# Tiles of a pair of source blocks and one target block in a graph network kernel, a dense stage without GpSimd, and other warm matmuls in the sort

## The reference, cut to what matters

```python
for l in range(5):                                   # L0
    h = leaky(x @ W1[l] + b1[l]) @ W2[l] + b2[l]
    e = leaky(edge_attr_32 @ We1[l] + be1[l]) @ We2[l] + be2[l]
    agg = segment_sum(h[src] * e * dot_scale[l], dst)
    x = layernorm(x + agg * res_w[l]) * ln_g[l] + ln_b[l]
# L1: rst = segment_sum((x * deg_out**-0.5) @ W [src], dst) * deg_in**-0.5 + bias
# L2 twice: softmax over the edges of a target, of q[dst].k[src], times v[src]
# last: segment_sum(relu(x[src] + edge_attr_64), dst)
```

## Time and profile before

| | us |
|---|---|
| median of 3 runs (8425.77 to 8462.65) | 8448.33 |
| the profiled execution, its own time | 8526.05 |
| its span | 8524.4 |

### The profile page before, as it was taken

How to read it: one execution, slowest core, us unless ns; L and a number is a source line. 1 busy time by engine, 2 the same in 40 slices (tenths; PEclk the granted TensorE clock), 3 DMA queues, 4 the chain that set the end, 5 groups by cost and what they waited for, 6 DMA issues and landing times. The chain is left out here.

```text
span 8524.4 us, 285239 instructions
## 1 busy us (share of the span) xinstructions
PE 6618.3 (78%) x79417; PEld 5068.7 (59%) x79424; DVE 6072.1 (71%) x17993; ACT 3076.6 (36%) x5080; POOL 3765.3 (44%) x5536
## 2 busy tenths in 40 slices
PE   5999999934444588788788787887777999999787
PEld 3555655623333467576566666665675777677676
DVE  7444444479999798789788798898554554455799
ACT  2443434412222444344343343343222333233344
POOL 2655666644443255355354454454994000000354
PEclk9888888865555798789798898888555999899999
DMA  3655555622222677577576576675232111111476
GB/s 85 168 163 158 164 163 164 168 54 56 57 57 56 193 174 176 129 176 175 131 175 165 139 175 151 154 175 145 104 116 84 67 64 44 60 69 63 109 191 168
DMA packets 1739057, 1083.39 MB, mean 127 GB/s; under 512 B 1256693, under 2 KB 1623980, under 8 KB 1729274
## 3 DMA queue, kind: packets, MB, share of 16 engines
q1 hardware_dynamic: 1105530, 739.41, 29.9%
q0 software_dynamic: 254336, 267.05, 13.7%
q10 hardware_dynamic: 379008, 74.48, 4.9%
HBM read 812.49 MB, written 266.72 MB: 127 GB/s over the span
## 5 line engine op out<-in xcount | busy, mean ns | idle before, releaser
L540 POOL DMA_DIRECT2D big<-rows x3384 | 1819.6, 538 | 3258.7 <-issue 2189.2
L1307 PE MATMUL ps<-big 128*128 128x64 bf16 x27072 | 1722.9, 204 | 528.8 <-DVE big L1753 312.8
L1307 PEld LDWEIGHTS ps<-big 128*128 128x128 bf16 x27072 | 1330.2, 102 | 890.4 <-issue 624.6
L810 POOL DMA_INDIRECT rows<-big x800 | 1007.6, 1260 | 754.3 <-ACT big L938 409.0
L1295 PE MATMUL ps<-big 128*128 128x64 bf16 x27072 | 1098.2, 202 | 102.2 <-DVE big L1768 41.3
L1295 PEld LDWEIGHTS ps<-big 128*128 128x128 fp8e4 x27072 | 988.6, 104 | 202.0 <-issue 145.5
L1034 ACT CAST big<-big 128x512 bf16<-128x512 f32 x940 | 581.2, 618 | 1153.5 <-DVE big L1781 1153.5
L1559 DVE SCALAR_TENSOR_TENSOR big<-big 128x1000 f32<-128x1000 f32 (+1 forms) x300 | 359.1, 1197 | 860.0 <-ACT big L923 603.5
L1040 ACT CAST big<-big 128x512 bf16<-128x512 f32 x1128 | 697.2, 618 | 586.6 <-issue 436.2
L1781 DVE TENSOR_TENSOR big<-ps,big 128x512 f32<-128x512 f32 x940 | 645.8, 687 | 275.2 <-PE ps L1295 261.8
L1256 PE MATMUL ps<-identb,big 128*128 128x128 bf16 x1504 | 341.4, 301 | 563.1 <-DVE big L1669 561.5
(11 more groups left out here) (259 smaller groups left out, 10337.1 us busy)
## 6 DMA issues: line engine op xcount, KB each, us to landing
big<-ohsD SPq DMA_DIRECT2D x564, 256.0 KB, 2.9
big<-ohdD SPq DMA_DIRECT2D x564, 256.0 KB, 3.5
big<-rows POOLq DMA_DIRECT2D x3384, 32.0 KB, 2.8
big<-rows SPq DMA_DIRECT2D x3384, 32.0 KB, 2.4
big<-maskD SPq DMA_DIRECT2D x50, 1600.0 KB, 6.6
big<-rows ACTq DMA_DIRECT2D x2256, 32.0 KB, 2.5
big<-keyT SPq DMA_DIRECT2D x100, 488.3 KB
maskD<-big SPq DMA_DIRECT2D x25, 1600.0 KB, 6.1
```

Of the source, the lines that this page charges most:

```text
L540: eng.dma_start(edge[:, s.r, j, :], rows[bass.ds(v[s.r * (hi - lo) + j - lo], P), col]).then_inc(landed[s.r], 16)
L810: pool.indirect_dma_start(out=rows[:, :], out_offset=bass.IndirectOffsetOnAxis(ap=sidx[0:EP, j, c:c + 1], axis=0), in_=stage[0:EP, j, c, : ...
L1307: last = pe.matmul(pacc[:, bass.ds(w[j], D)], hot[:, g.r, j * P:(j + 1) * P], parts[:, g.r, c, j * D:(j + 1) * D], start=False, stop=False ...
```

## The change

- **Tiles.** A bucket is now a pair of source blocks (VP = 13 pairs) and one target block. The formula for TILES gives 1152, so NG is 144 and there are 36 trips. The source id of an edge is its number among 256, and `ohS` is 256 columns wide (`iota1b` too). A table slice has 384 columns (two blocks by three parts); `tabq` gets a 26th block of zeros. A gather has two source one-hots per tile: 48 matmuls a group, in sums of six.
- **Counting.** TensorE turns both halves of `ohS` and multiplies 256 columns of counts per tile, which VectorE adds as 256 columns. The eight PSUM banks serve one group, so that each half waits for the same half of the group before. ScalarE makes four copies of 512 columns per group, with four semaphore counts. `ohD` has two buffers, not four. The first KEEP = 5 target one-hots of a group are stored and loaded, and MADE = 3 are remade.
- **Dense stage.** `find_over` goes to ScalarE as Relu(count - 65534), ahead by two block rows. VectorE multiplies that by the excess and adds it (one instruction), and the mask is the smaller of ln(2 count + tiny) and 1e28 times it; `make_far` goes. ScalarE keeps the even turns of a block row and VectorE the odd ones.
- **Sort.** One wide matmul of zeros ahead of each of the five outputs of a step, and twelve ahead of the first one in every fourth step; `be2p` is zeroed and the bias matmul goes over all 128 rows.

```diff
+VP = -(-W // 2)
+W2 = 2 * VP
+TILES = -(-((E + VP * W * (P - 1)) // P + VP * (QUAD - 1)) // 32) * 32
+KEEP = 5
+MADE = GT - KEEP
...
-        cmat = carve(W * W * P, dt=U16)
+        cpad = carve((W * W + 1) * P, dt=U16)
+        cmat = cpad[:, 0:W * W * P]
-        ohS = carve(2, GT, P, dt=BF16)
-        ohD = carve(RING, GT, P, dt=BF16)
-        ohsT = carve(2, GT * P, dt=U8)
+        ohS = carve(2, GT, 2 * P, dt=BF16)
+        ohD = carve(2, GT, P, dt=BF16)
+        ohsT = carve(2, 2 * GT * P, dt=U8)
...
-                sp.wait_ge(ohs_kept, i * 2 + 2)
+                sp.wait_ge(ohs_kept, i * 4 + 4)
...
-                sp.wait_ge(hots_ready, i * 2 + 1)
+                sp.wait_ge(hots_ready, i * 2 + 2)
...
-                             ohD[:, r, 0:QUAD, :].rearrange("p a b -> p (a b)")).then_inc(dst_stored[r], 16)
+                             ohD[:, r % 2, 0:KEEP, :].rearrange("p a b -> p (a b)")).then_inc(dst_stored[r % 2], 16)
...
-                sp.dma_start(hot[:, s.r:s.r + 2, 0:QUAD * P], ohdD[bass.ds(s.i, 2)].rearrange("g p f -> p g f")).then_inc(hot_loaded[s.r // 2], 16)
+                sp.dma_start(hot[:, s.r:s.r + 2, 0:KEEP * P], ohdD[bass.ds(s.i, 2)].rearrange("g p f -> p g f")).then_inc(hot_loaded[s.r // 2], 16)
...
+            def find_over(w, c):
+                act.wait_ge(craw_loaded[w % RAW], 16 * (w // RAW + 1))
+                if w >= 2:
+                    act.wait_ge(cfull_made, (w - 2) * CUTS + c + 1)
+                span = slice(c * CW, (c + 1) * CW)
+                act.activation(over_full[w % 2][:, span], craw[w % RAW][:, span], ACT.Relu, bias=step2[:, 2:3]).then_inc(over_made, 1)
+
...
-                act.activation(lnc[w % 2][:, span], cfull[w % 2][:, span], ACT.Ln, bias=tiny[:, 0:1]).then_inc(ln_made, 1)
+                act.activation(lnc[w % 2][:, span], cfull[w % 2][:, span], ACT.Ln, scale=2.0, bias=tiny[:, 0:1]).then_inc(ln_made, 1)
...
+                    elif w + 2 < W:
+                        find_over(w + 2, k - CUTS)
...
-                    for _ in range(12 if m == 0 else 0):
-                        pe.matmul(bank(4), zerob[:, :], each(iota1b[:, :], 4), start=True, stop=True)
-                    pe.matmul(to, onesb[0:3, 0:EP], be2p[0:3, p, :], start=True, stop=False, skip_group_check=True)
+                    for _ in range(12 if m == j == 0 else 1):
+                        pe.matmul(bank(4 + h), zerob[:, :], each(iota1b[:, 0:P], 4), start=True, stop=True)
+                    pe.matmul(to, onesb[:, 0:EP], be2p[:, p, :], start=True, stop=False, skip_group_check=True)
...
-                    if past(i, 2):
-                        pe.wait_ge(ohs_kept, i * 2 + (h - 3))
-                        pe.wait_ge(c_added[4 * h + 3], i - 1)
+                    if past(i, 1):
+                        pe.wait_ge(ohs_kept, i * 4 + (2 * h - 2))
+                        pe.wait_ge(c_added[4 * h + 3], i)
                     for j in range(4):
                         m = 4 * h + j
-                        pe.matmul(bank((r % 2) * 2 + h)[:, j * P:(j + 1) * P], ohS[:, r % 2, m, :], identb[:, :], start=True, stop=True)
-                        last = pe.matmul(bank(4 + (r % 2) * 2 + h)[:, j * P:(j + 1) * P], ohD[:, r, m, :], ohS[:, r % 2, m, :], start=True, stop=True)
+                        for k in range(2):
+                            pe.matmul(bank(2 * h + k)[:, j * P:(j + 1) * P], ohS[:, r % 2, m, k * P:(k + 1) * P], identb[:, :], start=True, stop=True)
+                        last = pe.matmul(bank(4 + 2 * h + j // 2)[:, j % 2 * 2 * P:(j % 2 + 1) * 2 * P], ohD[:, r % 2, m, :], ohS[:, r % 2, m, :], start=True, stop=True)
...
-                            for c in range(3):
-                                last = pe.matmul(pG[g.r][:, j * D:(j + 1) * D], ohsR[:, g.r, j * P:(j + 1) * P].bitcast(F8),
-                                                 slices[:, g.r, q // QUAD, c * D:(c + 1) * D], start=(c == 0), stop=(c == 2))
+                            for k in range(2):
+                                at = ((q // QUAD * 2 + k) * QUAD + j - q) * P
+                                for c in range(3):
+                                    last = pe.matmul(pG[g.r][:, j * D:(j + 1) * D], ohsR[:, g.r, at:at + P].bitcast(F8),
+                                                     slices[:, g.r, q // QUAD, (3 * k + c) * D:(3 * k + c + 1) * D],
+                                                     start=(k + c == 0), stop=(k + c == 3))
...
-                    if past(i, RING):
-                        dve.wait_ge(dst_stored[r], t * 16)
+                    if past(i, 2):
+                        dve.wait_ge(dst_stored[r % 2], t * 32 + 16 * (r // 2))
...
-                    own = cmat[:, bass.ds(two[r % 2 * GT + m] * P, P)]
+                    own = cpad[:, bass.ds(two[r % 2 * GT + m] * P, 2 * P)]
...
-                        last = dve.tensor_copy(slices[:, s.r, q, :], flat(tabq)[:, bass.ds(names[s.r * 2 + q], 3 * D)])
+                        last = dve.tensor_copy(slices[:, s.r, q, :], flat(tabq)[:, bass.ds(names[s.r * 2 + q], 6 * D)])
...
-                dve.tensor_tensor(lnc[w % 2][:, span], lnc[w % 2][:, span], far[w % 2][:, span], ALU.min).then_inc(mask_done, 1)
+                dve.scalar_tensor_tensor(lnc[w % 2][:, span], lnc[w % 2][:, span], STEEP, lnc[w % 2][:, span], ALU.mult, ALU.min).then_inc(mask_done, 1)
```

More of the change, by code:

```diff
@@ L268, in graph_kernel @@
         tres = carve(W, D)
-        tabq = carve(W, 3 * D, dt=BF16)
-        tabp = [tabq[:, :, c * D:(c + 1) * D] for c in range(3)]
-        slices = carve(RING, 2, 3 * D, dt=BF16)
-        ohsR = carve(RING, GT * P, dt=U8)
+        tabq = carve(W2, 3 * D, dt=BF16)
+        tabp = [tabq[:, 0:W, c * D:(c + 1) * D] for c in range(3)]
+        slices = carve(RING, 2, 6 * D, dt=BF16)
+        ohsR = carve(RING, 2 * GT * P, dt=U8)
         edge = carve(RING, GT, D)
@@ L287, in graph_kernel @@
         lnc = [carve(NP) for _ in range(2)]
-        far = [carve(NP) for _ in range(2)]
         ct = carve(CTS, 512)
@@ L366, in graph_kernel @@
         half_done = sem("half_done")
-        dst_stored = [sem(f"dst_stored{r}") for r in range(RING)]
+        dst_stored = [sem(f"dst_stored{r}") for r in range(2)]
         ohs_kept = sem("ohs_kept")
@@ L1092, in keep_counts @@
                     act.copy(ct[:, tau % CTS, 0:n], bank(tau % 4)[:, 0:n]).then_inc(ct_kept_a, 1)
+            for k in range(2 * CUTS):
+                find_over(k // CUTS, k % CUTS)
             for w in range(W):
@@ L1098, in _ @@
                         log_counts(w, k)
+                    elif w + 2 < W:
+                        find_over(w + 2, k - CUTS)
+                if w + 2 < W:
+                    for c in range(TURNS - CUTS, CUTS):
+                        find_over(w + 2, c)
             root(LAYERS + 2)
@@ L1382, in sum_rows @@
                 tau = w * TURNS + k
[L1383 removed]
+                kept(tau)
                 if k == 0 and w >= 2:
```

103 lines of the change are left out of this document (47 added, 56 removed).

## The result

The kernel after the change takes **7827.8 us** (median of 4 runs, 7812.4 to 7844.5) against 8440.9 (8425.8 to 8462.7) for the kernel before: ratio 0.927, 95% interval 0.924 to 0.930. The forecast was 7300, with 7020 to 7760: right in sign, 528 us too low.

What follows compares the result with a forecast made beforehand. Each stage had its own bounding engine; in passes TensorE would narrowly replace VectorE. Terms -618 (passes), -290 (sort), -251 (dense), +17 (counting), -18 (tables) sum to -1160: 8526 to 7366 profiled, 7300 median, range 7020 to 7760.

Steps and rivals of the forecast that it cites:

- The passes: Five layers and sixth pass: fewer groups (188 to 144) at 3.15 us each, -618 us in all (ends -840 and -230).
- I add the same 0.3: Pass period: 0.3 us for handing on and reading block numbers, added to TensorE's 2.8 us a group, giving 3.1.
- The feared loop: Passes: target one-hot load, the loop nearest its limit with about 1 us left, could make the period 3.4 us or more.
- The sort: Sort of the edges: fewer wide matmuls, a step of 13.3 us against 16.2, -290 us (ends -360 and +110).
- 14.8 - 2.76 + 7.75 x 0.23 = 13.8: Sort step in us: 14.8 from burst to burst, less the 2.76 burst, plus 7.75 wide matmuls at 0.23.
- the sort loses its clock: Rival, sort: half the time at 1.2 GHz, 17.3 us a step, +110 instead of -290, measured 7700; chance 0.15.
- The dense stage: Dense stage: GpSimd's two passes go, 11.5 us a block row against 21.6, -251 us (ends -299 and -164).
- The rule of the Trainium skill that I set against it: Dense stage: transposes do not raise the clock as other matmuls do; it might stay at 1.2 GHz, -164 for -251.
- Counting: Counting stage: 6.4 us a group including waiting for the target one-hot store, 922 us against 905, +17 (ends -20 and +100).
- Tables: Some 79 us of passes over TILES columns between sort and counting: 23% off, -18 us.
- The scaling: Whole kernel: median taken as 0.991 of the profiled time, turning 7366 us into 7300.
- a rival: Rival, passes at 1.2 GHz: 4.8 us a group, +740 instead of -618, about 8640, turning at 4.55; chance 0.04.

## Why the forecast was 528 us too low

- **The passes: -283 for -618.** The direction was right (TensorE becomes first, VectorE waits for gathers, clock 0.96), and so was the gather's 1.40 us. The step that failed is "I add the same 0.3" for handing on and reading block numbers, with "the scatter 1.39". That 0.3 was the slack of a period which VectorE paced, and says nothing of what TensorE's queue does in that time. Start to start, the kernel after has 1.40 for a gather, 1.54 for a scatter (1.39 in the sum) and 0.59 between them, the stalls: 3.53 a group in place of 3.1. In the mean of the six passes a group takes 3.54 us (514 of a layer's 570 us, if the rest of the layer takes the 56 it took before, and 486 in the sixth pass, each by 144 groups), 0.39 above the 3.15 that I took; by 864 groups that is the 335 us. Two removals of different things (the reads, or half the gather), worth 456 and 425 us, and one of a fifth of the bytes, worth nothing, show that TensorE's queue is the pace.
- **DMA.** The feared loop, the target one-hot load, isn't felt in the kernel after (4.1 us to land, against 2 x 3.5 of room). Once the reads are gone it is one of two limits behind TensorE: 61 us of waits in a pass, beside 44 for VectorE.
- **The sort: -133 for -290.** The step that failed is the pace of the step, built from TensorE's matmuls and its clock alone ("14.8 - 2.76 + 7.75 x 0.23 = 13.8"), with GpSimd as the only floor. The key loads aren't in it, nor the queue of SyncE in which they stand behind loads that wait for GpSimd. They landed in time at 16.4 us a step, and at 15 they are late in 42 of 100, and the stall shown above is followed by some 13 us at 1.2 GHz. With halved keys that are loaded four steps ahead the step is 13.41: 93 of the 156 us came with the halved keys and 63 with the four buffers. So a loop was missing. That 13.41 meets the forecast's 13.3 doesn't prove the sum of matmuls, since GpSimd is nearly full by then. The clock's own part: I expected over 0.93, got 0.85, and 0.91 without the stalls. The rival "the sort loses its clock" didn't come about, but the run with 3-row biases shows it at full size: it was one row count away. And the 133 us themselves don't need the sort's edit: 123 of them stay when it alone is undone, though in the kernel before the edit alone takes 100 off the profiled stage. Both would fit if much of the 133 is only that the profiles of before are of its longer executions; that is not shown.
- **The dense stage: -244 for -251.** Right, with 11.8 us a block row for 11.5. The reason is in part another: I had the three engines hand on to each other, with TensorE's matmuls at 8.1 us at 2.4 GHz or 15.0 at 1.2; it is busy 10.9 us a block row at clock 0.77, and the other two wait for it. The rule of the Trainium skill that I set against it ("TensorE: Matmul & The Clock Gate", Part 4, PE-mode transpose) would leave the stage at 1.2 GHz. The trace has neither that nor attention's 1.00: a third of this stage's small matmuls are transposes (625 of 1875), and the clock is 0.77.
- **Counting: -43 for +17.** The mis-sized term is the stall on the store of the target one-hots: I put 0.25 us a group on top of 6.15, and the wait for the store is 0.7 us over the whole stage. A group takes 5.98 us (860.9 / 144), so a tile takes 0.75 in the mean where I put 0.77 (0.69 from tile to tile within the timeline below). The -43 lies outside the ends that I gave for this term, -20 and +100.

```profile
2201.31 0.41 DVE L1701 TENSOR_TENSOR big<-big,ps 128x256 f32 x1
...
2202.00 0.41 DVE L1701 TENSOR_TENSOR big<-big,ps 128x256 f32 x1
```

- **Tables: -16 for -18**, right.
- **The scaling.** I took 0.991 between profile and median for the kernel after as well: -66 us. It didn't carry over (the median of after is 11 us above its profiled 7817, while the profile of before is of one of its three longer executions), which is 77 us of the miss. The other 451 are 1160 less the 709 measured: 335 + 157 - 60 + 7 + 2 = 441 by the terms, and 10 us in the stages that the table leaves out.
- **The range.** The passes and the sort stayed inside their own ends, but both came out on the slow side together, and with the scaling that is 68 us above 7760. The range took the terms as independent.
- **A slip in a rival.** At 4.8 us a group the six passes take 4147 us against 3342, so +805 and not +740, and the whole turns at 4.50 us a group and not 4.55. Nothing in the forecast hangs on it.

## What to carry to other kernels

Before an engine is made the pace, list everything that its queue does in a period, not only its busy time: register reads and unpacking cost little here under VectorE's pace, and 3.5 us a group instead of some 3.0 under TensorE's own. When a stage is to speed up by a tenth, walk every load issued a fixed number of steps ahead, find when its queue really issues it and what stands ahead of it there, and ask whether it lands in the new, shorter step. A gap of 0.3 us between a period and its busiest engine is no price for what another engine's queue does in that period. And a stage that got shorter has not shown that the edit made for it is the cause: undo the edit alone.

## What was not expected of the hardware

- A read of words into TensorE's registers costs by the word: 592 ns for eight and 1108 for sixteen, 65 ns a word, and no matmul is issued in the gap where it stands. Masking and shifting two numbers out of one word (an instruction of 32 ns, and the fused ones 58 instead of 37) lengthened a group's scatter by 0.44 us, more than the 0.26 us a group of reading the second words.
- Register instructions stand between the matmuls that they address: 24 matmuls take 1.5 us start to start with four ALU and eight 58-ns instructions, 1.06 with eight of 37 ns, 0.70 where nothing new is computed.
- A bias matmul of 3 rows and one of 128 take the same time at 2.4 GHz (375 and 379 ns), and the sort's clock was 0.65 with the one and 0.85 with the other. Why the rows count is not shown.
- A load's distance in steps is not its time to land. The key loads, meant two steps (30 us) ahead, were issued 15.7 us (median) after their buffer was free and landed 10.7 us later where they were waited for, 9.0 with half the bytes.
